# Count sets of layer 0 spread over its groups, three one-hot buffers, and another order around a layer's last groups

## What is computed

```python
def step(h, w):
    m = h @ w
    agg = jax.ops.segment_sum(m[src], dst, num_segments=n_nodes)
    gi = agg @ gru_wih.T + gru_bih
    gh = h @ gru_whh.T + gru_bhh
    ...
    r = jax.nn.sigmoid(ir + hr)
    z = jax.nn.sigmoid(iz + hz)
    n = jnp.tanh(i_n + r * h_n)
    return ((1.0 - z) * n + z * h, None)
```

## Time and profile before

| | us |
|---|---|
| median of 3 runs (lowest, highest) | 5637.86 (5631.97, 5638.38) |
| the profiled execution | 5632.32 |
| its span in the trace | 5630.6 |
| PE / DVE / ACT / POOL busy | 4788.8 / 2495.1 / 3705.4 / 4044.8 |
| first gather issue of layer 0's first stage | 169.4 |
| mean granted TensorE clock | 0.933 of full speed |

### The profile page before, as it was taken

How to read it: one execution, slowest core, us unless ns; L and a number is a source line. 1 busy time by engine, 2 the same in 40 slices (tenths; PEclk the granted TensorE clock), 3 DMA queues, 4 the chain that set the end, 5 groups by cost and what they waited for, 6 DMA issues and landing times.

```text
span 5630.6 us, 71035 instructions
## 1 busy us (share of the span) xinstructions
PE 4788.8 (85%) x21358; PEld 3523.9 (63%) x21358; DVE 2495.1 (44%) x7334; ACT 3705.4 (66%) x3174; POOL 4044.8 (72%) x4195
## 2 busy tenths in 40 slices
PE   5566666667887999999799999989999988999997
PEld 3333333335665877777677777767777767777775
DVE  7698888983333233333233333333333332333333
ACT  3465666665665877777577777666776766777774
POOL 2677777756775777777677777767777776777776
PEclk9788878878998999999899999999999999999998
DMA  5665555546668777778777777877777787777775
GB/s 187 210 203 190 190 184 191 190 163 213 210 208 265 225 226 228 226 227 262 235 225 226 218 231 222 278 220 218 225 222 221 220 281 217 208 217 218 212 218 152
DMA packets 830938, 1222.46 MB, mean 217 GB/s; under 512 B 88449, under 2 KB 656130, under 8 KB 823954
## 3 DMA queue, kind: packets, MB, share of 16 engines
q1 hardware_dynamic: 629888, 669.78, 39.0%
q0 software_dynamic: 200288, 546.90, 31.4%
q10 hardware_dynamic: 434, 1.81, 0.1%
HBM read 1031.88 MB, written 186.25 MB: 216 GB/s over the span
## 4 chain that ended last, share of the span: by engine, by line
POOL 63%; issue 21%; PE 8%; DMA 3%; DVE 2%; ACT 1%; POOLq 1%; DVEq 0%; SPq 0%; ACTq 0%
POOL messages L826 63%; PE four_ps L1835 3%; DMA messages<-table,src_stage 2%; PE agg_ps L1705 1%; DMA raw<-adjacency 1%; PE four_ps L1650 1%; PE four_ps L1776 0%; DVE gate_r L1193 0%; ACT counts L1020 0%; ACT room L981 0%; PE agg_ps L1712 0%; PE r_ps L1721 0%; PE r_ps L1658 0%; POOLq L149 0%; PE z_ps L1721 0%
## 5 line engine op out<-in xcount | busy, mean ns | idle before, releaser
L826 POOL DMA_INDIRECT messages<-table,src_stage x4151 | 4010.9, 966 | 1501.7 <-issue 1254.9
L1020 ACT ACTIVATE counts<-raw 128x2048 fp32r<-128x2048 uint8 x1624 | 2635.8, 1688 | 507.9 <-PE four_ps L1835 292.3
L1835 PE MATMUL four_ps<-counts,parts 128*128 128x512 f32 x11368 | 2795.4, 403 | 87.4 <-ACT counts L1020 71.7
L1835 PEld LDWEIGHTS four_ps<-counts,parts 128*128 128x128 f32 x11368 | 2150.3, 191 | 638.2 <-issue 177.9
L1292 DVE TENSOR_TENSOR selection<-agg_ps,dst_stage 128x1024 fp32r<-128x1024 bf16 x522 | 634.9, 1216 | 2430.2 <-PE agg_ps L1712 2428.5
L1705 PE MATMUL agg_ps<-messages,selection 128*128 128x256 f32 x4151 | 700.9, 316 | 344.9 <-DMA messages<-table,src_stage 337.8
L981 ACT ACTIVATE room<-four_ps 128x784 uint8<-128x784 f32 x832 | 638.1, 821 | 418.8 <-PE four_ps L1776 413.4
L1705 PEld LDWEIGHTS agg_ps<-messages,selection 128*128 128x128 f32 x4151 | 597.9, 207 | 402.2 <-DMA messages<-table,src_stage 333.6
L1776 PE MATMUL four_ps<-room 128*128 128x392 bf16 x1664 | 465.1, 394 | 296.2 <-DVE room L1427 166.6
L1426 DVE TENSOR_SCALAR room<-room 128x392 bf16<-128x392 f16 x1664 | 547.8, 329 | 70.0 <-PE four_ps L1776 54.5
L1776 PEld LDWEIGHTS four_ps<-room 128*128 128x128 bf16 x1664 | 124.4, 107 | 596.6 <-ACT room L981 369.7
(11 more groups left out here) (174 smaller groups left out, 2478.3 us busy)
## 6 DMA issues: line engine op xcount, KB each, us to landing
raw<-adjacency SPq DMA_DIRECT2D x812, 448.0 KB, 4.2
adjacency<-room SPq DMA_DIRECT2D x52, 1568.0 KB, 6.0
messages<-table,src_stage POOLq DMA_INDIRECT x4151
parts<-table SPq DMA_DIRECT2D x35, 1792.0 KB, 13.1
table<-table_stage SPq DMA_DIRECT2D x108, 512.0 KB, 3.0
h_old<-states SPq DMA_DIRECT2D x120, 256.0 KB, 5.1
states<-h_new SPq DMA_DIRECT2D x108, 256.0 KB, 4.7
table<-room SPq DMA_DIRECT2D x12, 512.0 KB, 3.0
```

Source lines behind the costliest of these rows:

```text
L826: nc.gpsimd.indirect_dma_start(messages[:, slot, t, :, :].rearrange("p i f -> p (i f)").bitcast(F32), None, table[k.layer % 2], bass.Indir ...
L1020: nc.scalar.activation(to, of, ACT.Copy).then_inc(expanded, 1)
L1835: last = mm(strip_ps, parts[:, block, half, :], counts[:, p % 2, at, :], start=(p == 0 and at == 0 and half == 0), stop=(p == PIECES - 1 a ...
```

## The change

In `building`, the 416 sets go over the first 97 of the 100 steps (`sets_to`: 4 or 5 sets each), none in the last three. The one-hot buffers are three (`HOTS`), and DVE is one set ahead at the start of each step. The loops over chunks are written out for PE, DVE, ACT and SP, so semaphore counts are constants and the `turns` increments go. SP issues the first five loads of `parts` at the start, one behind the other, instead of one before each quarter store of the first chunk. In `layers`, the six pieces done ahead stand in steps 85 to 87 (two each), and steps 88 to 91 have none. The last but one chunk's GRU parts 4 and later come one step earlier, so that its table product and its low halves stand at step 91. On PE the GRU parts of step 91 stand ahead of the final `sum_group`, and the final chunk's three products with the old state (`last_hidden`) as well; behind the final sum are left the products with `running`.

```diff
+def sets_to(step):
+    return min(SETS, -(-SETS * (step + 1) // (BUILD_STEPS - 3)))
@@ Stage
-        return LAYER_PIECES + (0 if self.layer == LAYERS - 1 else min(AHEAD[1], step + 1 - end))
+        return LAYER_PIECES + (0 if self.layer == LAYERS - 1 else min(AHEAD[1], 2 * (step + 1 - end)))
...
+            if chunk == LAST - 1 and t >= 3:
+                result += [(chunk, 3), (chunk, 4)] if t == 3 else [(chunk, t + 1)] if t < G_LAST else []
@@ SP building
+                for portion in range(QUARTERS + 1):
+                    load_portion(0, portion, LAST)
@@ DVE building
-                wait(dve, built, i * CHUNK_PAIRS + (a - 1) * SET_PAIRS)
+                wait(dve, built, (m - HOTS + 1) * SET_PAIRS)
...
+                for step in range(BUILD_STEPS):
...
+                    a, e = min(SETS, sets_to(step - 1) + 1), min(SETS, sets_to(step) + 1)
+                    middle = a + (e - a + 1) // 2
+                    for m in range(a, middle):
+                        one_hots(m)
+                    select_next(k, c, s, TAIL_GROUPS)
...
+                    for m in range(middle, e):
+                        one_hots(m)
+                add(k, LAST, TAIL_GROUPS - 1)
+                low_halves(k.v + EARLY - 1 + CHUNKS, J, r_ps)
@@ PE layers
+                    if step == LAYER_STEPS - 1:
+                        gru_steps(step)
+                        last_hidden(k.v + LAST)
                     sum_group(k, c, s)
...
-                    if step == LAYER_STEPS - 1:
-                        place_group(k, c, s)
-                    gru_steps(step)
-                    sum_pieces(k.pieces_at(step))
                     if step < LAYER_STEPS - 1:
-                        place_group(k, c, s)
+                        gru_steps(step)
+                        sum_pieces(k.pieces_at(step))
+                    place_group(k, c, s)
```

More of the change, by code:

```diff
@@ L217, in active @@
     def active(self, step):
-        return [(chunk, step - self.gru_at[chunk] + 1) for chunk in self.order if 1 <= step - self.gru_at[chunk] + 1 <= G_LAST]
+        result = []
+        for chunk in self.order:
+            t = step - self.gru_at[chunk] + 1
+            if chunk == LAST - 1 and t >= 3:
+                result += [(chunk, 3), (chunk, 4)] if t == 3 else [(chunk, t + 1)] if t < G_LAST else []
+            elif 1 <= t <= G_LAST:
+                result += [(chunk, t)]
+        return result
     def gathered(self, c, s):
@@ L612, in building @@
             def building(k):
[L613 to L625, removed]
                 sp.wait_ge(state_stored, 16 * CHUNKS)
                 sp.wait_ge(keys_out, KEY_BANKS)
[L629 to L639, removed]
+                for portion in range(QUARTERS + 1):
+                    load_portion(0, portion, LAST)
+                load_old(EARLY, J, 0, None)
+                for step in range(BUILD_STEPS):
+                    i, s = divmod(step, STEPS)
+                    v = i + (k.v - 1)
+                    for quarter in range(QUARTERS * DENSE_CHUNKS):
+                        if sets_to(step - 1) < (quarter + 1) * Q_PAIRS // SET_PAIRS <= sets_to(step):
+                            store_quarter(quarter)
+                    if s == 3 and i > 0:
+                        new_state(0, v, None, i + (EARLY - 1), J)
+                        load_old(i + EARLY, LAST_J if i + EARLY == LAST else J, 0, v)
+                    if s == 5 and i > 0:
+                        new_table(0, v, None, i + (EARLY - 1), J)
+                new_table(0, k.v + EARLY - 1, None, LAST - 1, J)
                 for u in range(2):
@@ L984, in building @@
             def building(k):
-                def iteration(i):
-                    has_gru = not (isinstance(i, int) and i == 0)
+                for step in range(BUILD_STEPS):
+                    i, s = divmod(step, STEPS)
                     v = i + (k.v - 1)
[L988 to L1004, removed]
+                    if i > 0 and s == 3:
                         candidate(v, J)
-                    for q in range(s * TAIL_SETS * SET_PAIRS, (s + 1) * TAIL_SETS * SET_PAIRS):
-                        count_edges(EARLY, q)
-                    if s == 1:
+                    for q in range(sets_to(step - 1) * SET_PAIRS, sets_to(step) * SET_PAIRS):
+                        count_edges(q)
+                    if i > 0 and s == 1:
                         gates(v, J)
-                make_table(v, J, r_ps)
+                    if i > 0 and s == 4:
+                        make_table(v, J, r_ps)
+                make_table(k.v + EARLY - 1, J, r_ps)
             def expand(k, i, p):
@@ L1817, in building @@
-                make_table(0, v, J, r_ps)
+                    sum_group(k, i + k.c0, s)
+                    if step == 0:
+                        place_group(k, k.c0 - 1, STEPS - 1)
+                    if i > 0 and s == 2:
+                        early_candidate(v, chunk_sum, h_old[0])
+                    for m in range(sets_to(step - 1), sets_to(step)):
+                        build_counts(m)
+                    if i > 0 and s == 1:
+                        early_gates(v, chunk_sum, (chunk_moved, i * 2 + 2 * k.moved), h_old[0], (h_loaded[0], i * 16 + 16 * k.old[0]))
@@ L1917, in gru_steps @@
                 def gru_steps(step):
-                    for chunk, t in k.active(step):
+                    for chunk, t in sorted(k.active(step), key=lambda entry: entry[0] != LAST):
                         n = k.order.index(chunk)
```

163 lines of the change are left out of this document (61 added, 102 removed).

## The result

The changed kernel takes 5601.44 us (median of 4 runs, 5593.96 to 5604.35), the kernel before took 5636.78 beside it: a ratio of 0.9936, 95% interval 0.9924 to 0.9949. Repeated on another chip (`e5`) it was 0.9941, 0.9927 to 0.9954. The profiled execution took 5593.96 us, the fastest of the four; its span is 5592.2.

The account below looks back on a forecast made before the run. The prediction took POOL's gathers, issued one behind the other, to bound the kernel. Its terms summed to -47.6 us from the profiled 5632.3, giving 5584.7 for such an execution and a median of 5590, likeliest range 5576 to 5613.

Parts of the forecast that it names:

- The gap: POOL's wait between layer 0's first and second stage shrinks from 56.6 to 10.5 us: -46 us.
- A dearer issue: Twenty sets moved beside first-stage gathers lengthen POOL's issues by 0.12 us a set: +2.4 us, at worst +47.
- 4.29 sets a step: The added 0.289 set a step in the first stage hides in PE's spare time: 0, at most +19 us.
- Written-out loops and the burst of loads: Loop branches removed beside POOL's time, and five portion loads issued at once: 0, bound +26 us.
- Layer ends: Three layer ends before another layer get about 2 us shorter each: -6 us, bounds -4 and +1 each.
- the bound named in the prediction: At a layer end, PE without pieces to multiply may run at the lower clock: up to +1 us each.
- The kernel's end: Chunk 23's decoder product and three old-state products now precede the last layer's last sum: +2 us, 0 to +4.
- the slipping pace: Rival: the added 0.289 set isn't hidden and POOL waits for PE in the first stage: 5609 us, chance 0.08.
- the gap moved: Rival: POOL starts stage 2 early but stands on its four buffers because strips can't start: about 5636 us, chance 0.04.
- the 12.0 us a step: Rival, slower: first-stage steps keep 2.8 us a set, against POOL's 10.6 us a step: 5726 us, chance 0.04.
- the port's case: Rival: each set moved beside first-stage gathers holds POOL while DVE is busy: +47, 5635 us, chance 0.04.

Follow-up runs that it names:

- e5: The changed kernel again, unedited, with more rounds on a second chip: 5611.39 us, where the kernel before took 5644.10.
- e2: The changed kernel with the old distribution of count sets (four a group, eight in each of the last four), all else kept: 5621.81 us, ratio 0.9977.
- e11: The changed kernel with the old distribution of sets, two one-hot buffers and no set ahead, on the slow chip: 6795.12 us, ratio 0.9952.
- e12: The changed kernel with two one-hot buffers and no set ahead, a repeat of e6 on the slow chip: 6755.36 us, ratio 0.9886.
- e3: The kernel before with only the `layers` part of the change, its first stage as before: 5636.29 us, ratio 1.0002.
- e7: The changed kernel with the last layer's order partly put back (final place ahead of the final chunk's GRU work): 5610.58 us, ratio 0.9940.
- e6: The changed kernel with two one-hot buffers instead of three and no set ahead, sets still spread: 5592.60 us, ratio 0.9908.
- e4: The changed kernel with nearly all one-hot operations left out after the first three sets, counts wrong: 5534.20 us, one execution.
- e8: The changed kernel with the 128-column one-hots left out but for one a set, counts wrong: 5579.60 us, one execution.
- e1: The changed kernel with two one-hot buffers instead of three, DVE still one set ahead: 5707.15 us, ratio 1.0129.
- e10: The changed kernel with three one-hot buffers but no set ahead, on the slow chip: 6702.00 us, ratio 0.9823.
- e9: The changed kernel with two one-hot buffers, no set ahead and the whole layer part taken back, on the slow chip: 6750.51 us, ratio 0.9900.

## Why the prediction was right, and what in it was not

**The total, 5590 forecast, 5601.4 measured**, inside the range of 5576 to 5613. The profiled execution is 9.3 us above the 5584.7 of the sum: 8.4 us of it is the dearer issue, the other terms come within about 1 us each. The median lies another 2 us higher above its profiled execution than was assumed.

**The gap, -46 forecast, -46.9 measured.** The chain was as worked out: sum, reduction, state of chunk 23, table product, low halves, index copy. `e2` (gap 48.2) and the pair `e11` and `e12` (81.0 and 28.3) show that it is the place of the sets that does most of it; 9.5 us also go without the spread, in `e2`.

**"A dearer issue", +2.4 forecast, +10.8 measured.** This is the mis-sized term. It charged 0.12 us for each of 20 sets more, as if a set's price were fixed. Some 6 us can be chance of one pair of profiles (`e3`), but `e5` and `e7`, with the same first stage, have 17.4 and 13.2 us in place of the 10.8, against the same profile of before. Per set built beside gathers (416 after, 395.5 before) the issues' durations carry, over 0.945 us each, 67.1 / 416 = 0.161 us, before 56.4 / 395.5 = 0.143, in `e6` 47.4 / 416 = 0.114. With `e6`'s price the term would have been below zero. What moves it is how many issues are held: 126 after, 82 before, 59 in `e6`. A piece of DVE and POOL rows of the changed kernel shows what that is:
```profile
837.98 1.27 POOL L833 DMA_INDIRECT messages<-table,src_stage  x1 [0.30 <-issue]
837.99 0.32 DVE L1417 TENSOR_SCALAR room<-room 128x392 bf16<-128x392 f16 x1
838.22 0.25 DVE L1418 TENSOR_SCALAR room<-room 128x128 bf16<-128x128 f16 x1
838.38 0.32 DVE L1417 TENSOR_SCALAR room<-room 128x392 bf16<-128x392 f16 x1
...
839.56 1.27 POOL L833 DMA_INDIRECT messages<-table,src_stage  x1 [0.30 <-issue]
839.57 0.32 DVE L1417 TENSOR_SCALAR room<-room 128x392 bf16<-128x392 f16 x1
...
841.13 1.17 POOL L833 DMA_INDIRECT messages<-table,src_stage  x1 [0.31 <-issue]
841.14 0.31 DVE L1417 TENSOR_SCALAR room<-room 128x392 bf16<-128x392 f16 x1
...
841.54 1.21 DVE L1283 TENSOR_TENSOR selection<-agg_ps,dst_stage 128x1024 fp32r<-128x1024 bf16 x1
842.61 0.95 POOL L833 DMA_INDIRECT messages<-table,src_stage  x1 [0.30 <-issue]
```
Each of the first two starts together with a large one-hot and lasts 0.32 us longer, one such operation; the third is longer by 0.22. Then 1.27 + 0.30 = 1.57 us is also four pairs of one-hots (four times 0.39), so the next issue starts in the same phase and is held too; the row ends where DVE does something else. Counted from 400 to 1190 us: of 139 issues that started within 0.05 us of a large one, 96 were held; of the other 451 only 4. Behind a held issue the next was held in 63% of cases, behind another in 8%. In `e6` it was 48 of 81 and 5 of 520, and 43% and 5%. The kernel before has 50 of 111 and 12 of 486, so such a start makes a hold likely and does not decide it. The difference to `e6`, 126 (149 in `e5`) to 59 held, times 0.32 us, is 21 to 29 us, against a pace difference of 20 to 26 us. The Trainium skill, "SBUF — State Buffer", section "Who interferes with whom", has a DVE tensor_scalar in a two-port mode and GpSimd lock each other out of a shared port pair for a whole instruction: the trace agrees as to the length of a single hold, 0.32 us, but not that every one-hot beside an issue holds it, and no run shows whether these one-hots are in such a mode. With `e4` it is shown that the one-hots make the excess; that the phase decides which issues are held rests on these counts alone. No run set the phase by itself, and `e8` speaks against it as a general rule: without most of the small one-hots only 5 of 68 issues with such a start were held, and 29 of the other 537.

**4.29 sets a step, 0 forecast.** Right as to pace by PE: POOL's waits for PE are 11.6 us. But half of my reason was wrong. I set the third buffer and the set ahead down as help against the 132.3 us that PE waited for one-hots. `e6` lacks both, PE waits 176.4 us there, and all that this costs is 5.4 us of a longer gap. On the calm chip the pair costs some 19 us in all. `e1` shows that the set ahead can't be had without the buffer; `e10` and `e12`, which differ in the buffer alone, show more held issues with it (15% to 8%), though it wins there. Whether the buffer without the set ahead beats `e6` on a calm chip wasn't tried, and why `e2`, with three buffers, had only 77 held issues is open.

**Written-out loops and the burst of loads, 0 forecast.** The first stage started 0.7 us later, and up to 300 us POOL waited for PE once, 0.3 us. `e11`, on the slow chip, has 0.9952 with the old sets, some of it perhaps these loops; not settled.

**Layer ends, -6 forecast, -5.6 measured** (-1.5, -0.4, -3.7), near the sum but not -2 each. That it is so near is luck: the same three ends were 21.7, 22.2 and 24.0 us in `e5`, 2.5 us less than before in all and not 5.6. At the end of layer 1 after the change:
```profile
2717.26 2.08 PE L1622 MATMUL four_ps<-w,h_new 128*128 128x128 f32 x8 [3.15 <-DVE h_new L1397]
2719.13 1.06 PE L1866 MATMUL r_ps<-h_old,w 128*128 128x256 f32 x2
...
2720.84 1.06 PE L1867 MATMUL four_ps<-h_old,w 128*128 128x256 f32 x2
2721.34 1.20 PE L1677 MATMUL agg_ps<-messages,selection 128*128 128x256 f32 x3
...
2724.16 0.70 PE L1873 MATMUL r_ps<-running,w 128*128 128x256 f32 x2 [0.51 <-DVE running L1331]
```
Windows of the some 22 us behind the last gather give the granted clock, of before and then of after, and the last row is a part of the latter:
```profile
2745.00:2768.00 23.00, 15.29 (x68) 12.38 (x67) 12.04 (x29) 7.73 (x11) 0.14 (x1) 0.89 0.59 183
```
```profile
2711.00:2733.00 22.00, 12.82 (x44) 9.07 (x45) 11.23 (x25) 6.36 (x9) 0.49 (x1) 0.68 0.48 149
...
2712.20:2722.40 10.20, 7.05 (x21) 5.07 (x19) 4.98 (x10) 1.32 (x2) 0.00 (x0) 0.50 0.45 134
```
That was the bound named in the prediction: for these 10.2 us the clock was at the lower of its two levels, 1.2 GHz, and the sum of three tiles took 1.20 us in place of 0.65, eight table products 2.08 in place of 1.64. The 3.15 us that PE idled, where the strip piece had stood, are not what brought it down, since they begin at 2714.12, after the fall; ahead of it PE had idled 1.26, 0.52 and 1.81 us in the 12 us from 2700. In all nine profiles with the new order on calm chips these ends have a mean clock of 0.58 to 0.86 in the 22 us from the last gather's start, before 0.85 to 0.93. That the missing pieces bring the clock down fits, but no run put them back alone. `e3` puts the whole layer part at nothing measurable, and `e9` against `e12` too.

**The kernel's end, +2 forecast, +2.2 measured**, and 28.0 to 29.1 us in every kernel with the new order on the calm chips. Here the size was right by the path that was named: the first product with `running` starts 14.5 us behind the last gather, before 12.2.

**The rivals.** POOL's waits for PE exclude the slipping pace, the next stage's pace of 1.259 (before 1.258) that the gap moved, and the 97 steps of 10.7 us the 12.0 us a step. POOL was never held for as long as DVE was busy, as the port's case had it, but the holds took back about a quarter of the gap that was closed (10.8 of 46.9 us).

**A version that beats both.** `e6`, the spread with two buffers, on a calm chip; on the slow chip, where the changed kernel itself wasn't run, `e10` was the fastest of four.

## What to carry to other kernels

Work that must follow an engine's last instruction belongs where that engine still runs; the last steps of a stage should be light. Price a buffer or head start by the engine that sets the time, not by the wait that it removes: here it took waits off PE, which had time, and added 0.3 us holds to POOL, which had none. Test each part of a bundle alone, and on more than one chip where a buffer's worth is in taking up pauses.

## What the runs showed that I had not expected

- Two engines can fall into step: POOL's held issue with its pause (1.57 us) is four pairs of DVE's one-hots, and holds come in rows (63% behind a held issue, 8% otherwise).
- Small one-hots matter too: without them the issues' excess fell from 67.1 to 40.7 us, and a start together with a large one held only 5 of 68 issues, where it had held 96 of 139.
- One chip ran the kernel before and the four others tried there some 20% slower, with pauses on all engines (of up to 12.8 us on POOL in `e12`) that the trace calls "issue"; the ratio of the spread alone stood (0.9886 and 0.9908). The third buffer gained 53 us there; on a calm chip it was tried only together with the set ahead, and the two lost 19.
